# A two-layer graph network on one core: how the turned state is stored, where the GRU's buffers lie, and in which order the last tiles are turned and the sums read out

## The reference, cut to what matters

```
h  = relu(layernorm(x))
x1 = x + conv3(relu(conv2(relu(conv1(h)))))          # layer 0
     conv(h): segment_sum((h @ W)[src] * norm, dst) + b

h   = relu(layernorm(x1))                             # layer 1
red = segment_sum(h[src] + relvectors[rel], dst)
out = x1 + GRU(red, h):
      gi = red @ w_ih.T + b_ih ; gh = h @ w_hh.T + b_hh
      r = sigmoid(i_r + h_r) ; z = sigmoid(i_z + h_z) ; n = tanh(i_n + r * h_n)
      (1 - z) * n + z * h
```

## Time and profile before

| | us |
|---|---|
| median of three runs | 884.1 (884.02 to 884.89) |
| the profiled execution | 879.43 |
| its span in the trace | 875.3 |
| TensorE busy | 834.1 (95%) |
| VectorE busy | 529.2 (60%) |
| ScalarE busy | 292.0 (33%) |
| GpSimd busy | 76.1 (9%) |

### The profile page before, as it was taken

One profiled execution on the slowest core, in us unless ns is written; L12 is line 12 of the kernel. 1 busy time (PEld: TensorE's weight loads), 2 busy tenths in 40 slices (PEclk: granted clock), 3 DMA queues, 4 the chain that ended last, 5 costly groups with the idle time before them and its releaser, 6 DMA issues.

```text
span 875.3 us, 14252 instructions
## 1 busy us (share of the span) xinstructions
PE 834.1 (95%) x4758; PEld 470.9 (54%) x4758; DVE 529.2 (60%) x1264; ACT 292.0 (33%) x602; POOL 76.1 (9%) x244
## 2 busy tenths in 40 slices
PE   2889999999999999999999999999998899999997
PEld 1457566666666445544554554554453455455554
DVE  8956999999997202101222545575666546574677
ACT  3365667677776111001111212221201213112233
POOL 0210110013000045550000000000000000000000
PEclk9989999999999999999999999999999999999999
DMA  6100000000000500000001213323704111111121
GB/s 203 32 2 1 4 17 23 17 17 22 18 23 17 175 3 3 3 3 1 0 5 37 76 35 85 89 74 97 171 16 136 47 48 48 33 36 43 55 73 57
DMA packets 77754, 40.38 MB, mean 46 GB/s; under 512 B 40460, under 2 KB 74973, under 8 KB 77677
## 3 DMA queue, kind: packets, MB, share of 16 engines
q1 hardware_dynamic: 77004, 38.98, 15.9%
q10 hardware_dynamic: 672, 0.41, 0.2%
HBM read 23.38 MB, written 15.63 MB: 45 GB/s over the span
## 4 chain that ended last, share of the span: by engine, by line
PE 80%; DVE 11%; SPq 3%; DMA 2%; issue 2%; ACT 2%; DVEq 0%; ACTq 0%
PE ps L1385 23%; PE ps L1046 13%; PE ps L1519 9%; PE ps L943 8%; PE ps L753 5%; PE ps L746 5%; PE ps L1410 3%; PE ps L1428 2%; PE ps L758 2%; PE ps L763 2%; PE ps L1018 2%; SPq L651 2%; DVE pair_a L1820 1%; DVE stats L1826 1%; PE ps L974 1%
## 5 line engine op out<-in xcount | busy, mean ns | idle before, releaser
L1046 PE MATMUL ps<-node_a,count 128*128 128x512 f16 x525 | 181.0, 381 | 1.6 <-DVE node_a L1153 1.1
L943 PE MATMUL ps<-node_b 128*128 128x175 f16 x808 | 162.1, 256 | 5.5 <-DVE node_b L295 3.5
L295 DVE TENSOR_TENSOR node_b<-node_b 128x1024 f16<-128x1024 f16 (+2 forms) x253 | 157.2, 669 | 0.0
L1241 ACT ACTIVATE count<-ps 128x500 f32 x202 | 122.8, 608 | 65.2 <-PE ps L943 59.6
L1385 PE MATMUL ps<-count,node_b 128*128 128x512 f16 (+2 forms) x700 | 133.2, 351 | 0.0
L1385 PE MATMUL ps<-count,node_a 128*128 128x512 f16 (+2 forms) x686 | 130.7, 351 | 0.0
L1385 PEld LDWEIGHTS ps<-count,node_b 128*128 128x128 f16 (+1 forms) x700 | 61.2, 97 | 70.9 <-issue 0.8
L943 PEld LDWEIGHTS ps<-node_b 128*128 128x128 f16 x808 | 79.5, 100 | 35.2 <-issue 7.0
L1385 PEld LDWEIGHTS ps<-count,node_a 128*128 128x128 f16 (+1 forms) x686 | 60.1, 98 | 69.2 <-issue 0.4
L1691 DVE SCALAR_TENSOR_TENSOR pair_a<-ps,dinv,params 128x256 f32<-128x256 f32 (+1 forms) x25 | 12.0, 479 | 122.2 <-PE ps L1410 122.2
L1519 PE MATMUL ps<-count,node_a 128*128 128x512 f16 x288 | 64.1, 379 | 0.0
(11 more groups left out here) (263 smaller groups left out, 957.0 us busy)
## 6 DMA issues: line engine op xcount, KB each, us to landing
table_scratch<-params SPq DMA_DIRECT2D x97, 32.0 KB, 1.7
node_a<-in_x SPq DMA_DIRECT2D x4, 768.0 KB, 8.1
count<-table_scratch SPq DMA_DIRECT2D x24, 128.0 KB, 2.1
table_scratch<-agg SPq DMA_DIRECT2D x21, 128.0 KB, 1.8
mixed_scratch<-node_b SPq DMA_DIRECT2D x10, 256.0 KB, 2.1
node_a<-mixed_scratch SPq DMA_DIRECT2D x4, 640.0 KB, 6.8
node_b<-table_scratch SPq DMA_DIRECT2D x3, 768.0 KB, 6.6
xt<-x_scratch SPq DMA_DIRECT2D x17, 128.0 KB, 2.1
```

What stands on the lines that cost most here:

```text
L295: return DVE.tensor_tensor(to, iota, keys.unsqueeze(2).to_broadcast([P, n, width, 2]), ALU.is_equal)
L943: return PE.matmul(window(s)[:, :, keys], low, key_hot[k][:, j, :, i].rearrange("p (t w) -> p t w", w=SPAN), start=(s == 0 and j == 0), st ...
L1046: last = PE.matmul(out_slot(u)[0:m, :], count[:, t, u * P:u * P + m], node_a[:, t, :, :].rearrange("p a d -> p (a d)"), start=(t == 0), st ...
L1241: ACTE.activation(to, window(s), ACT.Copy).then_inc(win_written, 1)
```

## The change

Six edits, which depend on one another through the buffers.

1. The turned state goes to a DRAM tensor of its own (`state_scratch`), as the 128 x 256 block that VectorE made: one DMA for a tile instead of four. The order of elements in DRAM is thus another, and the load takes it apart: four DMAs of 32 partitions a tile, each in runs of 32 floats (for the short tile eight).
2. The GRU's weights and the two biases of r and z lie in odd tiles of `count`; the biases of n, a gate buffer and the block sums of p = 1 lie in even ones; `h_t` and one `new_share` buffer lie in `pair_b`.
3. SP sends the weights after product B22 of p = 0 and step s3, ahead of the stores of the last four state tiles. Before it sent them after the last product, and these stores came first. The biases of n follow after T3.
4. VectorE turns the first two of the last four tiles before t2, the other two after c12, ahead of t3, c21 and c22.
5. ScalarE copies the first half of a chunk's sums before the norm of the chunk before it, and the second half inside that norm, after its first pair.
6. TensorE waits for c22 before the first GRU tile of a p instead of behind it.

```diff
-        PIECES = 13
-
-        def freed(k, n=1):
-            return count[:, k:k + n, 0:FREED].bitcast(F32)
-
-        w_ih_rz, w_ih_n = freed(0, 2), freed(2)[:, 0, :].rearrange("p (f d) -> p f d", f=HALVES)
-        w_hh_all, w_hh_rz, w_hh_n = freed(3, 3), freed(3, 2), freed(5)[:, 0, :].rearrange("p (f d) -> p f d", f=HALVES)
-        bias_rz, bias_rz2 = freed(6)[:, 0, :], freed(8)[:, 0, :]
-        bias_in, bias_hn = freed(9)[:, 0, 0:D], freed(9)[:, 0, D:2 * D]
-        h_t = [freed(10)[:, 0, k * D:(k + 1) * D].rearrange("p (f n) -> p f n", f=HALVES) for k in range(2)]
-        gate_rz = [freed(7)[:, 0, :], bias_rz2]
-        new_share = [bias[0], freed(12)[:, 0, 0:D]]
-        x1_tile = [xt[0][:, :], xt[1][:, :], freed(11)[:, 0, 0:D]]
-        h_tile = [scaled[0], scaled[1], freed(11)[:, 0, D:2 * D]]
+        PIECES = 16
+
+        def freed(t, n=1):
+
+            return count[:, t:t + 2 * n - 1:2, 0:FREED].bitcast(F32)
+
+        w_ih_rz, w_ih_n = freed(1, 2), freed(5)[:, 0, :].rearrange("p (f d) -> p f d", f=HALVES)
+        w_hh_all, w_hh_rz, w_hh_n = freed(7, 3), freed(7, 2), freed(11)[:, 0, :].rearrange("p (f d) -> p f d", f=HALVES)
+        bias_rz, bias_rz2 = freed(13)[:, 0, :], freed(15)[:, 0, :]
+        bias_in, bias_hn = freed(2)[:, 0, 0:D], freed(2)[:, 0, D:2 * D]
+        h_t = [pair_b[:, 4 + 2 * k:6 + 2 * k, :] for k in range(2)]
+        gate_rz = [freed(0)[:, 0, :], bias_rz2]
+        new_share = [bias[0], pair_b[:, 2:4, :].rearrange("p a d -> p (a d)")]
+        block_sums_b = [freed(t)[:, 0, :] for t in (8, 10, 12, 14)]
+        x1_tile = [xt[0][:, :], xt[1][:, :], freed(4)[:, 0, 0:D]]
+        h_tile = [scaled[0], scaled[1], freed(4)[:, 0, D:2 * D]]
...
-        h_dram = table_dram.rearrange("n d -> (n d)")
 
         def blocks(t):
             return -(-rows(t) // BLOCK)
 
         def stores_of(order, i):
 
-            return h_stored[i % 2], 16 * sum(blocks(order[n]) for n in range(i % 2, i + 1, 2))
-
-        def turned_rows(t):
-            return h_dram[t * P * D:t * P * D + D * rows(t)]
+            return h_stored[i % 2], 16 * (i // 2 + 1)
+
+        def state_rows(t):
+            return h_dram[t * P * D:t * P * D + blocks(t) * BLOCK * D]
 
         def state_store_sp(order, i):
 
             t = order[i]
             SP.wait_ge(state_turned, i + 1)
-            to = turned_rows(t).rearrange("(j c n) -> c j n", c=BLOCK, n=rows(t))
-            for b in range(blocks(t)):
-                nodes = slice(b * BLOCK, min((b + 1) * BLOCK, rows(t)))
-                SP.dma_start(to[:, :, nodes], h_blocks[i % 2][b * BLOCK:(b + 1) * BLOCK, :].rearrange("c (j n) -> c j n", n=BLOCK)[:, :, 0:nodes.stop - nodes.start]).then_inc(h_stored[i % 2], 16)
+            SP.dma_start(state_rows(t).rearrange("(p d) -> p d", d=D), h_blocks[i % 2][0:blocks(t) * BLOCK, :]).then_inc(h_stored[i % 2], 16)
+
+        STATE_LOADS = P // BLOCK
+
+        def loads_of(order, i):
+
+            return h_in[i % 2], 16 * STATE_LOADS * sum(1 if rows(order[n]) == P else HALVES for n in range(i % 2, i + 1, 2))
 
         def state_load_sp(order, i):
-            m = rows(order[i])
-            SP.dma_start(h_t[i % 2][:, :, 0:m], turned_rows(order[i]).rearrange("(f p n) -> p f n", p=P, n=m)).then_inc(h_in[i % 2], 16)
+            t = order[i]
+            of = state_rows(t).rearrange("(b c f j n) -> j c f b n", c=BLOCK, f=HALVES, n=BLOCK, j=STATE_LOADS)
+            for j in range(STATE_LOADS):
+                to = h_t[i % 2][j * BLOCK:(j + 1) * BLOCK, :, :].rearrange("c f (b n) -> c f b n", n=BLOCK)[:, :, 0:blocks(t), :]
+                for f in [slice(0, HALVES)] if rows(t) == P else [slice(f, f + 1) for f in range(HALVES)]:
+                    SP.dma_start(to[:, f, :, :], of[j][:, f, :, :]).then_inc(h_in[i % 2], 16)
...
+        def gru_biases_sp():
             SP.dma_start(bias_in, spread(b_ih[2 * D:G])).then_inc(gru_b_in, 16)
             SP.dma_start(bias_hn, spread(b_hh[2 * D:G])).then_inc(gru_b_in, 16)
...
-                PE.wait_ge(h_in[k], 16 * (i // 2 + 1))
+                PE.wait_ge(*loads_of(order, i))
...
             tail_pe(p, B21, 0, 0).then_inc(product_done, 1)
             PE.wait_ge(rest_out, 2)
+            PE.wait_ge(*block_out_at(p - 1, "c22"))
             gru_pe(n)
-            PE.wait_ge(*block_out_at(p - 1, "c22"))
...
             step_dve(0, "s4")
+            for t in last[:2]:
+                state_dve(t)
             block_dve(0, "t2")
             step_dve(0, "s3")
             block_dve(0, "c12")
-            for t in last[:2]:
+            for t in last[2:]:
                 state_dve(t)
             for k in range(XS):
                 DVE.wait_ge(x1_out[k], 16 * len(range(k, T, XS)))
             for which in ("t3", "c21", "c22"):
                 block_dve(0, which)
-            for t in last[2:]:
-                state_dve(t)
...
             for i, c in enumerate(chunks):
+                cols = min(CHUNK, N - c * CHUNK)
+                ACTE.wait_ge(conv_done, 2 * T + done_before[i])
+                sums_act(h0 + HALVES * i, agg[:, 0, :], cols, scales[:, 4:5])
                 if i:
-                    norm_act(chunks[i - 1])
-                    ACTE.wait_ge(conv_done, 2 * T + done_before[i])
+                    norm_act(chunks[i - 1], lambda: sums_act(h0 + HALVES * i + 1, agg[:, 1, :], cols, scales[:, 4:5]))
                 else:
-                    ACTE.wait_ge(conv_done, 2 * T)
-                for f in range(HALVES):
-                    sums_act(h0 + HALVES * i + f, agg[:, f, :], min(CHUNK, N - c * CHUNK), scales[:, 4:5])
-            norm_act(chunks[NC - 1])
+                    sums_act(h0 + 1, agg[:, 1, :], cols, scales[:, 4:5])
+            norm_act(chunks[NC - 1], None)
...
+                between()
                 return
...
                 ACTE.activation(far_of(i)[:, :, 0, :], pair[:, NEAR:NEAR + FAR, :], ACT.Copy).then_inc(pair_high, 1)
+                if between and i == of[0]:
+                    between()
...
                 for t in tiles_of[c]:
-                    state_store_sp(order, place[t])
+                    if c != chunks[-1]:
+                        state_store_sp(order, place[t])
+            SP.wait_ge(*product_at(0, B22))
+            SP.wait_ge(*step_at(0, "s3"))
+            gru_weights_sp()
             for k in range(XS):
                 SP.wait_ge(x1_out[k], 16 * len(range(k, T, XS)))
-            SP.wait_ge(*product_at(0, "last"))
-            gru_weights_sp()
-            gru_begin_sp(gru_order)
+            for i in range(2):
+                gru_load_sp(gru_order, i)
+            for t in tiles_of[chunks[-1]]:
+                state_store_sp(order, place[t])
+            for i in range(2):
+                SP.wait_ge(state_turned, T)
+                SP.wait_ge(*stores_of(order, place[gru_order[i]]))
+                state_load_sp(gru_order, i)
+            SP.wait_ge(*product_at(0, T3))
+            gru_biases_sp()
+            gru_load_sp(gru_order, 2)
             for i in (T - 2, T - 1):
                 SP.wait_ge(*stores_of(order, i))
-            for i in range(2):
-                state_load_sp(gru_order, i)```

The instruction streams show what moves. First SP, from the stores of the last four state tiles to the first loads of the GRU; before:

```order
L651 DMA table_scratch<-params 32x8x32 x16
L668 DMA count<-in_L_gnn_w_ih 128x2x512
L669 DMA count<-in_L_gnn_w_ih 128x2x256
L668 DMA count<-in_L_gnn_w_hh 128x2x512
L669 DMA count<-in_L_gnn_w_hh 128x2x256
L670 DMA count<-in_L_gnn_b_ih 128x512
L671 DMA count<-in_L_gnn_b_hh 128x512
L672 DMA count<-in_L_gnn_b_ih 128x256
L673 DMA count<-in_L_gnn_b_hh 128x256
L659 DMA xt<-x_scratch 128x256 x2
L659 DMA count<-x_scratch 128x256
L655 DMA count<-table_scratch 128x2x128 x3
```

More of the change, by code:

```diff
@@ L2314 @@
     table = nc.dram_tensor("table_scratch", shape, mb.dt.float32, kind="Internal").ap()
+    state = nc.dram_tensor("state_scratch", (-(-shape[0] // P) * P * shape[1],), mb.dt.float32, kind="Internal").ap()
     mixed = nc.dram_tensor("mixed_scratch", (10, 128, 1024), mb.dt.float16, kind="Internal").ap()
```

9 lines of the change are left out of this document (4 added, 5 removed).

## The result

| | before | after |
|---|---|---|
| median, 4 runs each on one chip, us | 884.06 (883.29 to 884.89) | 870.87 (870.01 to 872.94) |
| ratio | | 0.9854 [0.9834, 0.9874] |
| the profiled execution, us | 879.43 | 871.41 |
| its span, us | 875.3 | 866.9 |
| mean granted clock of TensorE in it | 0.992 | 0.991 |

The change makes the kernel 13.2 us faster by medians. By the two profiled executions it is 8.0 us (8.4 by their spans). The prediction said 9.6 for both, so it erred to one side on the traces and to the other on the medians. That difference is what most of the experiments are about.

The account below looks back on a forecast made before the run. TensorE, busy 834.1 of 875.3 us, was taken as the bound. Gaps and slow clock of 11.96 us less a 2.4 us stall gave 9.56: 884.1 to 874.5 us, 8-in-10 range 871.2 to 879.5.

Parts of the forecast that it names:

- the five gaps that go: TensorE waits before 499.54, 614.32, 633.86, 675.60 and 681.22 us: 1.89, 2.85, 0.28, 1.73 and 3.66 us, all to go.
- the stall that comes: TensorE's T3 tail waits for VectorE's t3, held by state stores behind 2 MB of weights: 2.4 us, bounds 0 and 4.
- the term for slow clock: Four matmuls (L753) behind the 3.66 us gap run at 1.2 GHz: 1.55 us to be won.
- a clock of 1.00 all through: Sign of a right forecast: gru_pe(0) starts with no gap and TensorE's granted clock stays at 1.00.
- Read-out split: ScalarE copies sums around the previous chunk's norm; gaps of 1.89 and 2.85 us go: gain 4.74 us, price 0.
- the stores: One store a tile, 4 of 128 KB for 16 of 32 KB: earlier norm of the last chunk, 0.28 us gained.
- Weights sooner: SP sends GRU weights 16 us ahead; both first GRU tile gaps and slow clock go: 1.73 + 3.66 + 1.55 = 6.94 us.
- The fit that the prediction quotes: A DMA takes 2.0 us plus bytes over 436 GB/s: 2.5 MB through in 7.7 us; not used for the sum.
- Tile loads: Four state-load DMAs a tile on SP, issues of 0.45 us and landing of 1.9: 3.7 us, hidden under 7.5.
- the rival "slower": GRU tile loads pass one after another, 9.4 us each: 7.5 to 22.5 us more, up to 897 us; chance 0.08.
- the stall-free case: Small stores get through in time, no stall before the T3 tail: 872.1 us; chance 0.18.
- the long stall: Stores land at 667, T3 tail stalls 5.5 us, clock halves again (1.55): 879.2 us; chance 0.16.

Follow-up runs that it names:

- the trace at 884 us: Third trace of the kernel before, unchanged, a single profiled execution: 884.05 us, span 879.8, clock 0.986.
- The filled kernel: Kernel before with dummy matmuls of 512 columns added in TensorE's gaps, every wait kept: 879.49 us against 883.46, ratio 0.9956.

## Why the prediction was partly wrong

The direction, the five gaps that go and the stall that comes were right. The time, 874.5, was too high, and the 870.87 measured lies below the range, which began at 871.2. The step that failed is the term for slow clock. The prediction counted 1.55 us of it, behind the 3.66 us gap, nothing behind the shorter ones, and said of the stall "A stall of this length costs no clock", from the 3.7 us of the sixteen matmuls behind the 2.85 us gap. That row was one execution, and at that place the luckier kind. In an execution of 884 us, the time from which the prediction subtracts, the term measures about 4.6: 1.5 in the GRU, as counted, and 3.1 behind the two L1410 gaps. The sign "a clock of 1.00 all through" failed too, with 0.54 and 0.60 behind the stall.

- **From 9.6 to 13.2 us.** The prediction carried the profiled execution's saving to a median 4.7 us above it, as if those 4.7 us were a constant beside the gaps. In the trace at 884 us 3.1 of them are slow clock behind the two L1410 gaps (1.6 and 1.5), and these go with the gaps; 1.5 lie ahead of the first gap. 9.56 and 3.1 make 12.7, where 13.2, 12.7 and 11.4 were measured in three series. The scatter is that of before's executions, and the 13.2, from four of them all at 883 or more, is at its upper end. The filled kernel bears the size out by itself: 4.0 us in all at the median, of which the prediction had 1.55.
- **From 9.56 to 8.0 us on the two traces.** The stall was 2.16, not 2.4 (0.2 better), and 1.7 us of slow clock stood behind it (worse). Together they give 8.1.
- **Read-out split.** Predicted 4.74 at price 0. Both gaps went. In the changed kernel it brings 8.2 us, the gaps and their clock; alone it brought nothing, since the next gap, 0.28 before, grew to 3.26 and another of 0.99 came. The prediction saw that VectorE's norm ends just where TensorE would arrive (630.3 to 631.3 against 630.73), and there the traces agree: in after, where all this lies some 2 us earlier, node_a is ready at 628.40 and TensorE starts at 628.50. But it booked 4.74 to the split by itself and 0.28 to the stores, when the split alone has no value that can be told. That the single stores are what lets it count is read from the waits; they were not run by themselves.
- **Weights sooner.** Predicted 6.94; the gaps went, but the early send earned little of it. With the old sending order 0.77 of the 5.39 us of gaps came back. The rest is that SP was no longer held 5.2 us past the last product by late turning and small stores. The prediction knew that sixteen stores held SP 9.23 us in the chunk before, and priced only what they cost the norm.
- **The stall.** The prediction had t3 done at 664.85 in the clock of before. B22's tail, at 651.68 before, is at 646.32 after, 5.36 us sooner, so that is 659.5 in after; it was done at 658.67 + 0.71 = 659.4. The two stores, predicted at 663.0 and 663.6, that is 657.6 and 658.2 here, landed at 657.8 and 658.2. The order of events and the sum of transfers held. Its bounds, 0 and 4 us, left out the clock. The fit that the prediction quotes from the Trainium skill, DMA: Bandwidth & Descriptors (Anatomy of one DMA), is given there for DMAs that GpSimd issues; these are SP's, and after's six weight and bias DMAs (2 MB) took 9.9 us from the first issue, at 646.95, to the last landing, 7.2 behind 649.64.
- **Tile loads.** Predicted 3.7 us from issue to landing. The four issues took 2.54 us at 850 us, 0.6 each instead of 0.45, and a load landed 2.1 us later (median of 85): 4.6 us, still under 7.5, so hidden. Even eight loads a tile opened no wait; the rival "slower" did not come near.
- **Rivals.** Neither the stall-free case (872.1) nor the long stall held. What was missing was the case that the median's distance from the trace belongs to the gaps in good part.

What stays open: why the same gap is followed by slow clock in one execution and not in the next. The traces, taken together, have these gaps on TensorE after 440 us (the filled ones left out, and those under 0.9 us, none of which was followed by it):

| gap, us | gaps | followed by slow clock |
|---|---|---|
| 0.99 to 1.90 | 8 | 0 |
| 1.98 to 2.85 | 9 | 6 (1.98, 2.00, 2.07, 2.16, 2.54, 2.65; not 2.13, 2.24, 2.85) |
| 3.26 to 4.29 | 5 | 5 |

In the middle row length alone doesn't sort them. Why the first 100 us vary in clock between executions, which is worth 1.5 us between two traces of before, was not studied.

## What to carry to other kernels

Compare the mean clock and the time of the profiled execution with those of the timed runs before you sum up gaps. When they differ, ask whether the difference is part of the gaps' price: here 3.1 of 4.6 us were, and a gap of 2 to 3 us on TensorE cost its length plus 1.5 to 1.8 us in six of nine cases. Edits that each shorten a wait of the same chain should be priced together, and then each with the others left out, since the first alone may only move the gap. And ask of each edit what the others already do for it: with the other edits in place the early weights had 0.77 us left to save, and together with the early turning they brought a stall of 1.5 to 2.2.

## What the runs showed of the hardware

- TensorE was at 1.2 GHz behind idle times of 1.98 to 2.65 us, for up to some 4 us and 1.5 to 1.8 us of loss, in some executions and not in others. The kernel's times spread over 6 to 7 us with such gaps and over 2 when dummy matmuls fill them. The Trainium skill, TensorE: Matmul & The Clock Gate (Part 1), says of the slow phase at a kernel's start that it is run-variable; here that holds for gaps in the middle too.
- Two 128 KB stores behind 2 MB of loads on SP's queue landed after 4.9 and 5.5 us, where four without them took 1.7 to 2.0. How long SP itself is held there varies: the issues of the two x1 loads between took 2.00 us in after's first trace, 0.80 in its second and 1.60 in its third.
- DMAs of 32 KB in 128-byte runs landed in 2.1 us (median of 85; 1.5 to 3.8), hardly longer than 32 KB stores (1.7), at 0.6 us of issue each.
